# Twenty-eight row places and one-hot places in place of fourteen, with TensorE's loop over 28 tiles, in a graph attention kernel

## The reference

```python
def gat_layer(x, W, a_src, a_dst, bias, src, dst, heads, out_c, concat):
    n = x.shape[0]
    h = (x @ W).reshape(n, heads, out_c)
    al_s = jnp.einsum('nhc,hc->nh', h, a_src)
    al_d = jnp.einsum('nhc,hc->nh', h, a_dst)
    e = jax.nn.leaky_relu(al_s[src] + al_d[dst], NEG_SLOPE)
    m = jax.ops.segment_max(e, dst, num_segments=n)
    ex = jnp.exp(e - m[dst])
    z = jax.ops.segment_sum(ex, dst, num_segments=n)
    alpha = ex / (z[dst] + 1e-16)
    out = jax.ops.segment_sum(h[src] * alpha[:, :, None], dst, num_segments=n)
    ...
h = elu(gat_layer(ln(x), W1, ..., heads=8, out_c=96))
x = x + gat_layer(h, W2, ..., heads=1, out_c=768)
x = x + experts(ln(x))
```

## Time and profile before

| | before |
|---|---|
| median of 3 runs | 2661.32 us (2656.72 to 2662.03) |
| profiled execution, its own time | 2677.26 us |
| its span in the profile | 2675.5 us |
| aggregation of layer 0 | 553.6 to 1149.7 us |
| aggregation of layer 1 | 1563.5 to 2149.3 us |
| busy share of the span: PE, DVE, ACT, POOL | 73%, 48%, 26%, 44% |
| granted clock of PE over the span | 0.895 |

### The profile page before, as it was taken

The page is one execution under the profiler, slowest core; times in us unless marked ns, Lnnn a source line. Parts: engine busy times, 40 slices in busy tenths (PEclk is TensorE's granted clock), DMA queues, the critical chain, the costliest instruction groups (busy, mean ns, idle before and its releaser), DMA issues. The chain is left out here.

```text
span 2675.5 us, 35096 instructions
## 1 busy us (share of the span) xinstructions
PE 1958.1 (73%) x9881; PEld 1101.3 (41%) x9882; DVE 1294.4 (48%) x2945; ACT 696.6 (26%) x1757; POOL 1189.2 (44%) x1236
## 2 busy tenths in 40 slices
PE   2746778967777777755577967777777768898985
PEld 1324545533333333333344532222222256666664
DVE  7625657656666666666476004344343436211111
ACT  2500101211111111143122334334443343233332
POOL 5065653046666666611411146666666600233433
PEclk9868888988999899978799988898888877899998
DMA  5322321268888888876686788888888868466665
GB/s 181 96 57 57 82 54 35 89 208 277 280 278 282 274 275 278 284 251 160 177 207 162 204 264 298 302 296 296 297 302 299 296 204 310 89 123 124 122 124 89
DMA packets 166262, 540.77 MB, mean 202 GB/s; under 512 B 37841, under 2 KB 47036, under 8 KB 165922
## 3 DMA queue, kind: packets, MB, share of 16 engines
q0 software_dynamic: 91392, 377.70, 49.1%
q1 hardware_dynamic: 60242, 122.30, 13.8%
q10 hardware_dynamic: 14544, 39.82, 3.8%
HBM read 452.70 MB, written 87.01 MB: 202 GB/s over the span
## 5 line engine op out<-in xcount | busy, mean ns | idle before, releaser
L1697 PE MATMUL acc<-ring,work 128*64 128x384 f32 (+1 forms) x880 | 213.8, 574 | 89.5 <-issue 71.5
L1467 PE MATMUL acc<-ring,work 128*64 128x384 f32 x880 | 216.3, 574 | 71.2 <-issue 55.7
L901 PE MATMUL acc<-wg,work 128*128 128x384 f32 x600 | 231.9, 531 | 26.9 <-issue 19.5
L1218 PE MATMUL acc<-wg,work 128*128 128x384 f32 x600 | 215.1, 507 | 23.8 <-ACT work L1275 20.7
L1606 POOL DMA_INDIRECT ring<-feat_tab,src_t x196 | 185.4, 946 | 104.6 <-issue 46.9
L1414 POOL DMA_INDIRECT ring<-feat_tab,src_t x196 | 185.2, 945 | 104.7 <-issue 45.0
L1782 ACT ACTIVATE work<-big,edges 128x64 f32<-128x64 f32 x392 | 135.9, 427 | 341.7 <-DMA edges<-in_w_slow 326.0
L851 POOL DMA_INDIRECT edges<-score_tab,src_p x168 | 165.5, 985 | 126.9 <-PE tps L889 55.7
L1471 PEld LDWEIGHTS acc<-edges,work 128*64 128x64 f32 x882 | 127.3, 147 | 188.8 <-issue 182.1
L1444 DVE TENSOR_TENSOR ring<-ring,mps 128x768 f32<-128x768 f32 x196 | 179.4, 950 | 46.4 <-DMA ring<-feat_tab,src_t 36.3
L1665 DVE COPY work<-acc 64x384 f32<-64x384 f32 x100 | 55.9, 559 | 297.4 <-DMA edges<-in_w_slow 261.8
(11 more groups left out here) (384 smaller groups left out, 3665.6 us busy)
## 6 DMA issues: line engine op xcount, KB each, us to landing
feat_tab<-work ACTq DMA_DIRECT2D x50, 384.0 KB
ring<-lo_rows SPq DMA_DIRECT2D x49, 256.0 KB
edges<-in_w_slow SPq DMA_DIRECT2D x28, 384.0 KB, 5.3
edges<-in_w_hebb POOLq DMA_DIRECT2D x28, 384.0 KB, 7.4
edges<-in_w_fast POOLq DMA_DIRECT2D x28, 384.0 KB, 8.5
unit_sum<-edges SPq DMA_DIRECT2D x28, 384.0 KB, 5.5
out_rows<-ring ACTq DMA_DIRECT2D x26, 384.0 KB
agg_raw<-work ACTq DMA_DIRECT2D x25, 388.0 KB
```

Of the source, the lines that this page charges most:

```text
L901: m = nc.tensor.matmul(acc[:, sl * 2 + c, 0:C // 2], xT[sl][:, k, :], wg[:, k, c * (C // 2):(c + 1) * (C // 2)], start=(k == 0), stop=(k = ...
L1218: m = nc.tensor.matmul(acc[:, sl * 2 + c, 0:C // 2], xT[sl][:, k, :], wg[:, k, c * (C // 2):(c + 1) * (C // 2)], start=(k == 0), stop=(k = ...
L1467: m = nc.tensor.matmul(acc[c * WIN:(c + 1) * WIN, bank, 0:CHUNK], hot, row[:, c * CHUNK:(c + 1) * CHUNK], start=start, stop=True, skip_gro ...
L1697: m = nc.tensor.matmul(acc[c * WIN:(c + 1) * WIN, bank, 0:n], hot, row[:, c * CHUNK:c * CHUNK + n], start=start, stop=True, skip_group_che ...
```

## The change

- `RING` is 28: fourteen more row places, in `big`, and 28 semaphores `row_in` in each layer. POOL waits for `tile_mm` of t - 28 + 2 from the twenty-ninth gather on.
- The one-hots have 28 places (`HOTS` = 4 batches), at the end of `big`. In layer 0 DVE makes batch n + 1 ahead of the messages of batch n, where it made batch n there; the wait for a batch's places is for `batch_mm` of n - 2 in place of n (for batch n). In layer 1 ACT's wait is loosened in the same way.
- In layer 1, L1637 writes ones behind 28 row places in place of 14.
- PE's loop has 14 turns of 28 tiles written out, in place of 28 turns of 14. The word of bits is loaded twice in a turn.

```diff
-RING = 14
+RING = 28
+HOTS = 4
 UN = 14
 BATCH = 7
@@
-        onehot = agg_part(UN * WIN).rearrange("p (a n) -> p a n", a=UN)
+        onehot = big[:, KC * NP - RING * WIN:KC * NP].rearrange("p (a n) -> p a n", a=RING)
@@ aggregate
-            rows = msg_rows + [edges[:, j * ROW:(j + 1) * ROW] for j in range(RING - len(msg_rows))]
+            rows = msg_rows + [edges[:, j * ROW:(j + 1) * ROW] for j in range(UN - len(msg_rows))] + [big[:, j * ROW:(j + 1) * ROW] for j in range(UN)]
@@ POOL, the same in both layers
-                        k = t % UN
-                        if t >= UN:
-                            pool.wait_ge(tile_mm, t - UN + 2)
+                        k = t % RING
+                        if t >= RING:
+                            pool.wait_ge(tile_mm, t - RING + 2)
@@ DVE, layer 0
-                    def hots(i, j):
-
-                        first = i * UN + j * BATCH
-                        if i > 0:
-                            dve.wait_ge(batch_mm, i * 2 + j)
-                        V.tensor_tensor(onehot[:, j * BATCH:(j + 1) * BATCH, :], near.to_broadcast([P, BATCH, WIN]),
+                    def hots(n):
+
+                        first, at = n * BATCH, n % HOTS * BATCH
+                        if n >= HOTS:
+                            dve.wait_ge(batch_mm, n - HOTS + 2)
+                        V.tensor_tensor(onehot[:, at:at + BATCH, :], near.to_broadcast([P, BATCH, WIN]),
@@
-                            dve.wait_ge(row_in[k], i * 16 + 16)
-                            r3 = rows[k][:, 0:C].rearrange("p (h c) -> p h c", h=H)
+                            r = i % 2 * UN + k
+                            dve.wait_ge(row_in[r], i // 2 * 16 + 16)
+                            r3 = rows[r][:, 0:C].rearrange("p (h c) -> p h c", h=H)
@@
                     for i in range(TURNS):
                         for j in range(2):
-                            if i > 0:
-                                hots(i, j)
+                            if i * 2 + j > 0 and i * 2 + j + 1 < 2 * TURNS:
+                                hots(i * 2 + j + 1)
                             if j == 1 and i < TURNS - 1:
                                 weights(i + 1)
                             messages(i, j)
@@ PE, the same in both layers
                         if k % BATCH == 0:
-                            pe.wait_ge(hot_ready, i * 2 + (k // BATCH + 1))
+                            pe.wait_ge(hot_ready, i * HOTS + (k // BATCH + 1))
@@
-                        t = i * UN + k
+                        t = i * RING + k
@@
-                        with pe.If((bits & (1 << k)) > 0):
+                        with pe.If((bits & (1 << k % UN)) > 0):
@@
-                    with pe.Fori(0, TURNS) as i:
-                        pe.load(bits_reg, open_bits[0:1, ds(i, 1)])
-                        bits = pe.snap(bits_reg[0], min_val=0, max_val=(1 << UN) - 1)
-                        for k in range(0, UN, 2):
-                            with pe.If((bits & (3 << k)) > 0):
+                    with pe.Fori(0, TURNS // 2) as i:
+                        for k in range(0, RING, 2):
+                            if k % UN == 0:
+                                pe.load(bits_reg, open_bits[0:1, ds(i * 2 + k // UN, 1)])
+                                bits = pe.snap(bits_reg[0], min_val=0, max_val=(1 << UN) - 1)
+                            with pe.If((bits & (3 << k % UN)) > 0):
                                 single(i, k, bits)
                                 single(i, k + 1, bits)
@@ ACT, layer 1
-                            if i > 0:
-                                act.wait_ge(batch_mm, n)
+                            if n >= HOTS:
+                                act.wait_ge(batch_mm, n - HOTS + 2)
```

More of the change, by code:

```diff
@@ L1447, in _ @@
                     dve.wait_ge(ex_set, 1)
-                    hots(0, 0)
-                    hots(0, 1)
+                    hots(0)
+                    hots(1)
                     weights(0)
@@ L1530, in _ @@
                                 with pe.If(bank > 0):
-                                    added(i, k, i * UN + k, 1)
-                                    added(i, k + 1, i * UN + (k + 1), 1)
+                                    added(i, k, i * RING + k, 1)
+                                    added(i, k + 1, i * RING + (k + 1), 1)
                                 with pe.Else():
-                                    added(i, k, i * UN + k, 0)
-                                    added(i, k + 1, i * UN + (k + 1), 0)
+                                    added(i, k, i * RING + k, 0)
+                                    added(i, k + 1, i * RING + (k + 1), 0)
                     close()
@@ L1593, in aggregate_rows @@
             part = spot(1)
-            rows = msg_rows + [spot(ROW) for _ in range(RING - len(msg_rows))]
+            rows = (msg_rows + [spot(ROW) for _ in range(UN - len(msg_rows))]
+                    + [big[:, 2 * NT + 2 * BATCH * WIN + j * ROW:2 * NT + 2 * BATCH * WIN + (j + 1) * ROW] for j in range(UN)])
             assert at[0] <= 2 * NT * 8
@@ L1778, in _ @@
                             act.wait_ge(apart, n + 1)
-                            if i > 0:
-                                act.wait_ge(batch_mm, n)
+                            if n >= HOTS:
+                                act.wait_ge(batch_mm, n - HOTS + 2)
                             for k in range(BATCH):
-                                ins = nc.scalar.activation(onehot[:, j * BATCH + k, :], gaps[j][:, k, :], ACT.Relu,
+                                ins = nc.scalar.activation(onehot[:, n % HOTS * BATCH + k, :], gaps[j][:, k, :], ACT.Relu,
                                                            bias=ex[:, first + k:first + k + 1],
```

## The result

The changed kernel takes 3075.37 us (median of 3 runs, 3067.95 to 3080.90) against 2661.32: the ratio is 1.156, with a 95% interval of 1.152 to 1.160. The forecast had the sign and the mechanism, but 126 us where 414 came, outside its range.

What follows compares the result with a forecast made beforehand. No engine full, transfers nearest, POOL pausing for row places; afterwards PE's code fetches bind. Profiled execution 2677.3 + 102 + 27 - 3 = 2803 us; for the median 2661.3 + 126, rounded 2788 us; range 2615 to 2980.

Steps and rivals of the forecast that it cites:

- the tails: Time from last gather to each aggregation's end, 10.8 and 7.3 us before: expected to shorten, taken as 3 us gained.
- Step (3): PE's doubled loop code doesn't stay and is fetched again in each of 14 passes: +102 us layer 0, +27 layer 1.
- The price of a packet: PE's stall for each fetched packet of loop code: 1.4 us taken in both layers, bounds 0.68 and 2.2.
- The cover: All PE idle time hides code fetches: 10.9 us a pass in layer 0, 11.4 in layer 1; without window changes, 6.3 and 6.8.
- The clock: PE's granted clock, 0.92 and 0.88, may fall if PE idles more; 0.85 in layer 0 would cost 35 us.
- Step (2): POOL's pauses for free row places, 189 us, shrink with a deeper ring: about 60 us gained at the weak end, 159 strong.
- The first rival: Longer gather runs win: code stays or its fetch hides, POOL's pauses shrink; 2600 us, bounds 2500 and 2658, chance 0.19.
- the second rival: Fetches hide but POOL's pauses stay, runs set by PE's progress when counts are delivered: 2661 us within 5, chance 0.06.
- The strong end of the gain: All POOL pauses go and DMA binds, at most about 0.99 busy: 159 us gained over both layers.
- Step (1): DVE's waits before one-hot batches, 124.0 us in layer 0, mostly go; costed at nothing, as is ACT in layer 1.
- Steps (4) and (5): Fourteen more memsets before layer 1's first gather: 0.2 us, at most 0.9; second load of bits in a turn: nothing.
- the third rival's case: Code fetches cost more, window changes no cover or packet nearer 2.2 us: +258 us and up, 2919 or more; 0.15 of slower's chance.

Runs made afterwards that it cites:

- The doubled loop alone: Kernel before with only PE's loop changed to 14 turns of 28 tiles in both layers, 14 places kept: 3032.3 us (1.134); on another chip 3032.9 us (1.141).
- the padded loops: Kernel before plus never-executed products in PE's loop: 8.4/8.5 packets (layer 0/1) 1.364, 7.8 in both 1.446, 7.1/7.0 1.156.
- the loop padded to 8.4 packets: Kernel before plus 9 (layer 0) and 17 (layer 1) products per tile in a never-taken branch: 3649.8 us, 1.364.
- the loop of 14 tiles without pair programs: Kernel before, 14 places, without separate programs for pairs that have no window's end; each tile takes the `single` program: 2687.2 us, 1.005.
- the trace with 28 places: Changed kernel without the separate programs for pairs lacking a window's end: 2823.4 us, 1.054 of the kernel before; its layer 1 took 609.6 us.
- half rows: Kernel before, each gather bringing 384 numbers instead of 768, with as many gathers, products and counts: 0.998, 0.997 and 0.998 on three chips.
- counts for every second tile: Kernel before, but PE counts up `tile_mm` only behind every second tile and POOL waits for the pair: 1.000 in each of three measurements.

## Why the prediction was wrong

The sum said +102 us for layer 0, +27 for layer 1 and -3 for the tails. The profile shows +270.2 and +121.7. (Its last sum, 2661.3 + 126, is 2787 and not 2788, which changes nothing.)

**Step (3), the code, was right in kind.** The loop doesn't stay, and each pass fetches it. That it doesn't was assumed; the runs show it for this loop and for those of 7.8 packets and more. 13 and 9.5 packets a pass were forecast, 194 / 14 = 13.9 and 152 / 14 = 10.9 measured. The doubled loop alone shows that it is this part of the change, the padded loops that it is the size of the code. What failed is the sizes of the terms: a packet's price, what idle time covers, and the clock, left out of the sum.

**The price of a packet, the term that failed first.** I took 1.4 us from the first pass of the kernel before. It is 340 / 194 = 1.75 us in layer 0 and 251 / 152 = 1.65 in layer 1, inside the bounds of 0.68 and 2.2 but above what the sum uses. A single stall is 340 / 116 = 2.9 us on average, longer than the 2.2 that I took for a whole one (layer 1 had already shown 3.29): the first pass had two in each layer, and none of them was the jump back over the whole loop, 61 / 13 = 4.7 us. With the packets' number this is 340 - 14 x 18.2 = 85 us in layer 0 and 251 - 14 x 13.3 = 65 in layer 1; the price alone is 194 x 0.35 = 68 and 152 x 0.25 = 38 of it.

**The cover, the second.** I counted all of PE's idle time as cover, 152.2 and 159.2 us. It took up 340 - 213.5 = 126 us in layer 0 and 251 - 139.9 = 111 in layer 1, so 26 and 48 us less. The bound without the window's changes, 6.3 and 6.8 us for a pass, was too low, 14 x 6.3 = 88 and 14 x 6.8 = 95, so the cover lies between the two bounds. No run shows which idle time served as cover; the 126 and 111 us are what is left when the growth of PE's idle time is taken from its stalls.

**The clock, the third.** I named a fall to 0.85 at 35 us and kept it out of the sum. It fell to 0.78 in layer 0, and PE's busy time grew by 57 us. In layer 1 it fell from 0.88 to 0.81, and the busy time fell by 18. The trace's clock records part this. They have two levels, full speed and half of it. PE was busy at the half for 248 us in layer 0 and 153 in layer 1, where it had been 81 and 116; a product of 384 columns takes 868 ns in layer 0 there and 506 at full speed. By an estimate from these, the clock cost 167 x (1 - 506 / 868) = 70 us and 37 x 0.42 = 15. The remaining busy time fell by 13 and 33 us. The kernel before carries such a surplus on chips of this kind, 42 and 48 us against the quick kind (last section), and the changed kernel doesn't: 500.6 and 408.4 us here, 494.0 and 413.0 there. Why PE is busier there stays open. In layer 0 the clock was 0.92 with 152.2 us of PE's idle time before, 0.78 with 365.7 in the changed kernel, and 0.71 with 524.3 in the loop padded to 8.4 packets. I read it so that idling lowered the clock and cost PE twice; small differences don't follow this, as 0.96 with 168.8 us in the loop of 14 tiles without pair programs.

Together: 102 + 85 + 26 + 57 = 270 and 27 + 65 + 48 - 18 = 122. As the cover is what was left, this closes by construction and proves nothing by itself.

**Step (2) and the tail.** -3 us was the wrong sign. When PE binds, the places fill up: 27 tiles stand gathered behind the last gather, and PE works them off alone. That was +24.6 us by the medians on one chip. In the profiled executions it was 38.5, the tails' growth of 41.3 less what earlier gathers won. It is no further term of the sum above but lies within PE's busy and idle time, so a part of the missing cover may be this. Even with code that stays, the places gain nothing: 1.484 and 1.487 us apart, and 15 us lost. The first rival had assumed that a pause in a longer run costs less for each gather, from the first runs of the trace; the second rival, that a run is set by how far PE has come, is what the trace with 28 places shows, 392 / 87 = 4.5 gathers in a run with 28 places and 392 / 95 = 4.1 with 14, except that it left out the tail. The sum had left this gain out, so the miss doesn't come from it; the 0.19 for the first rival rested on it. The strong end of the gain assumed DMA engines busy at 0.99 at most, which was my estimate: the kernel before shows 0.94 and, from 1563.5 to 1578.5 us, 0.96, and the runs show 0.96 over a whole aggregation (last section).

**Step (1).** I expected DVE's waits before its one-hots, 124.0 us, to go. They grew, since all wait for PE now:

```profile
  PE acc L1469: 413.4, 46
```

It cost nothing, as forecast: with PE binding, DVE's idle time was free here.

**Steps (4) and (5)** can't be seen in the total: POOL's first gather of layer 1 waited 0.4 us for the memsets where 0.3 is usual, and the stretches between and behind the aggregations are as long as before within 2 us.

The chance of 0.75 for slower was fair. The range was not: its upper end lay 60 us above the third rival's case, whose price rested on the same two stalls of the first pass. With my own upper bound of 2.2 us for a packet and all idle time as cover, the sum gives 14 x (28.6 - 10.9 + 20.9 - 11.4) = 381 us, so about 3040, which the range left out.

## What to carry to other kernels

Count the instructions of TensorE's hardware loop before writing more of it out. Here, by my estimates of their sizes, loops of up to 7.0 packets of 16,384 bytes stayed, of 7.1 and 7.2 the first fell out and the second stayed, and those of 7.8 and more were fetched whole in every pass. A loop of 8.4 packets, much of which is jumped over, cost more than twice what the doubled loop did, as it is passed 28 times and not 14: some 10 packets a pass at 1.7 us each. The limit is shown only as lying between 7 and 8 packets, and whether the loop's place within a packet decides between 7.1 and 7.2 is not shown. Within loops of 4.8 to 7.2 packets that stayed, PE branched without a fetch behind the first pass.

A deeper ring gained nothing in any run here: where the consumer sets the pace, it only moved work behind the last transfer, and with code that stays it left the pace of the gathers as it was. And a price taken from a few events of a first pass was too low here: the jump that repeats, back over the whole loop, was not among them.

## What the runs showed of the hardware that was not expected

The kernel before takes 11 to 12% longer in three of the six groups than in the other three. In the quick ones, 2384 to 2387 us, gathers come 1.25 us apart in the traces (of half rows and of counts for every second tile; the kernel before itself was profiled in the first group only); in the others they come 1.46 to 1.50 us apart. The kernel with counts for every second tile was profiled on both kinds; first the quick one:

```profile
474.00:973.10 499.10, 393.64 (x2750) 204.49 (x2748) 399.64 (x476) 67.89 (x196) 371.01 (x392) 0.94 0.93 328
1362.20:1858.60 496.40, 371.64 (x1868) 141.87 (x1865) 230.16 (x652) 234.91 (x782) 371.11 (x392) 0.93 0.96 350
```

then the other:

```profile
558.30:1148.70 590.40, 435.35 (x2750) 215.81 (x2748) 399.68 (x476) 67.33 (x196) 371.41 (x392) 0.93 0.84 278
1560.00:2139.00 579.00, 419.85 (x1868) 159.19 (x1866) 226.07 (x639) 234.96 (x782) 371.71 (x392) 0.90 0.88 300
```

The aggregations are 174 of the 283 us between these two executions; the rest lies outside them, as the first gather at 474.0 and not at 558.3 us shows. Within them the granted clock is nearly the same, but PE is busy for 42 and 48 us more, and its counts arrive later. ACT's wait for a closed window ends, on the quick chip, with PE's closing product:

```profile
  PE tps L1477: 398.3, 49
```

and on the other with an event that the profile can't tie to one, as in the earlier trace rows:

```profile
  remote: 445.1, 45
```

From the end of the closing product to ACT's copy it takes 0.04 us in the median on the quick chip and 5.6 on the other; the kernel before has 6.4 in the first group. The changed kernel in that same group has 0.10, and so have the doubled and the padded loops in layer 0, where code is fetched in each pass. So on chips of the slower kind late counts go together with gathers that are issued one behind another, and are mostly gone where fetches hold PE back and POOL waits for it. Which is the cause was not tested.

The pauses that I took for a property of the kernel, worth 60 us or up to 159, come and go with the chip. On the quick kind they don't exist, and POOL's issuing, 392 x 1.25 = 490 us of the 499.1 and 496.4, sets the time.
